# Roots by small steps on GpSimd, no product part in a short turn, and turned tokens cast by VectorE, in the second layer of a gated cross-attention block

## The reference

```python
def _L1_xattn_ref(x, context, Wq, Wk, Wv):      # 32 heads of 8
    def _rmsnorm(t):
        return t * jax.lax.rsqrt(jnp.mean(t * t, axis=-1, keepdims=True) + 1e-6)
    q = x @ Wq.T
    k_raw, v_raw = context @ Wk.T, context @ Wv.T
    ...
    q, k = _rmsnorm(q), _rmsnorm(k)
    attn = jax.nn.softmax(jnp.einsum('bhnd,bhmd->bhnm', q, k) * 8 ** -0.5, axis=-1)
    return jnp.einsum('bhnm,bhmd->bhnd', attn, v)
```

## Time and profile before

| | |
|---|---|
| median of three runs | 1718.73 us (1718.09 to 1726.04) |
| profiled execution | 1721.58 us, its span 1719.8 us |
| TensorE (PE) busy | 1616.0 us, 94% of the span |
| VectorE (DVE) busy | 1393.7 us, 81% |
| ScalarE (ACT) busy | 1381.0 us, 80% |
| GpSimd (POOL) busy | 1273.5 us, 74% |
| mean granted TensorE clock | 0.983 |
| feed-forward stage and first tiles | about 1200 to 1302 us |
| layer 1's attention and last half | 1302 us to the end |

### The profile page before, as it was taken

One profiled execution on the slowest core, in us unless ns is written; L12 is line 12 of the kernel. 1 busy time (PEld: TensorE's weight loads), 2 busy tenths in 40 slices (PEclk: granted clock), 3 DMA queues, 4 the chain that ended last, 5 costly groups with the idle time before them and its releaser, 6 DMA issues. The chain is left out here.

```text
span 1719.8 us, 43340 instructions
## 1 busy us (share of the span) xinstructions
PE 1616.0 (94%) x16022; PEld 1011.1 (59%) x16022; DVE 1393.7 (81%) x3487; ACT 1381.0 (80%) x2317; POOL 1273.5 (74%) x1170
## 2 busy tenths in 40 slices
PE   3799999999999999999999999988998999999997
PEld 1466777767776677767777777766553333333332
DVE  8889999999999989999888888889995755555422
ACT  4688888788888788888888888873337999999996
POOL 3558778787787877887877787765896989989400
PEclk9899999999999999999999999998999999999998
DMA  4299989999999999999989999996323232222100
GB/s 175 87 177 203 195 206 205 195 205 222 202 189 200 190 198 185 224 211 207 196 194 218 217 194 209 211 186 175 104 44 108 44 77 39 44 39 45 26 14 14
DMA packets 608867, 261.07 MB, mean 152 GB/s; under 512 B 576528, under 2 KB 581648, under 8 KB 607248
## 3 DMA queue, kind: packets, MB, share of 16 engines
q1 hardware_dynamic: 604432, 258.05, 70.3%
q10 hardware_dynamic: 4224, 0.25, 0.2%
HBM read 99.15 MB, written 17.29 MB: 68 GB/s over the span
## 5 line engine op out<-in xcount | busy, mean ns | idle before, releaser
L1750 PE MATMUL pv<-PT,VV 128*128 128x256 bf16 (+1 forms) x2880 | 340.6, 275 | 12.1 <-DMA PT<-PB 12.1
L1730 PE MATMUL score<-KK,QT 128*128 128x512 bf16 (+2 forms) x1920 | 341.5, 322 | 6.5 <-DVE mxp L1225 6.5
L2316 POOL TENSOR_TENSOR l_rr<-l_rr,mhalf 128x32 f32<-128x32 f32 (+1 forms) x60 | 333.2, 5553 | 5.0
L1490 ACT ACTIVATE PB<-S,rsum 128x1024 bf16<-128x1024 f32 (+1 forms) x256 | 246.5, 988 | 106.0 <-DVE rsum L1256 81.6
L1750 PEld LDWEIGHTS pv<-PT,VV 128*128 128x128 bf16 (+1 forms) x2880 | 280.7, 99 | 79.9 <-issue 31.8
L1247 DVE SCALAR_TENSOR_TENSOR PB<-S,rsum,PB 128x1024 bf16<-128x1024 f32 (+1 forms) x256 | 297.6, 1163 | 3.1 <-ACT PB L1490 3.1
L1730 PEld LDWEIGHTS score<-KK,QT 128*128 128x128 bf16 x1920 | 158.1, 98 | 144.0 <-DVE mxp L1225 12.6
L1480 ACT ACTIVATE S<-S,nmx 128x1601 f32<-128x1601 f32 x128 | 210.2, 1643 | 7.2 <-DVE nmx L1237 7.0
L2582 ACT ACTIVATE P<-score 128x1024 f32<-128x1024 f32 x196 | 199.1, 1060 | 12.6 <-PE score L2674 5.9
L1068 POOL TENSOR_SCALAR S<-S,rsum 128x256 f32<-128x256 f32 x128 | 73.1, 571 | 129.8 <-DVE rsum L1256 116.2
L2694 PE MATMUL pv<-P,V 128*9 128x256 f32 (+1 forms) x2288 | 154.2, 384 | 3.8 <-DVE pv L2120 2.4
(11 more groups left out here) (264 smaller groups left out, 3577.6 us busy)
## 6 DMA issues: line engine op xcount, KB each, us to landing
x<-rs_d SPq DMA_DIRECT2D x16, 936.0 KB, 5.3
rsb<-rs_d SPq DMA_DIRECT2D x16, 936.0 KB, 5.5
wsb<-w_split SPq DMA_DIRECT2D x46, 256.0 KB, 4.7
wsb<-w_split SPq DMA_DIRECT2D x23, 512.0 KB, 4.9
wpr<-in_wprojT SPq DMA_DIRECT2D x23, 512.0 KB, 6.5
context_d<-stage SPq DMA_DIRECT2D x16, 400.2 KB, 3.7
l_ctx<-context_d SPq DMA_DIRECT2D x4, 1601.0 KB, 7.2
rawh<-in_w_all SPq DMA_DIRECT2D x12, 512.0 KB, 5.5
```

Source lines behind the costliest of these rows:

```text
L1490: e.activation(m.PB[n % 2][:, 2 * a:a + b], m.S32[n % 2][:, a:b], ACT.Copy, scale=m.rsum[n % 2][:, 1:2]).then_inc(s["p_hi"], 1)
L1730: i = e.matmul(m.score[:, at:at + b - a], qt[:, kind, qp, q * P:(q + 1) * P], kk[:, kp, a:b], start=(k == 0), stop=(k == 2))
L1750: i = e.matmul(m.pv[:, at:at + 256], vv[0:rows, v, t, :], m.PT[k % 2][0:rows, turned(c, a), :], start=(c == first and r == 0), stop=(c == ...
L2316: e.tensor_tensor(rr, rr, m.mhalf[0:rows, 0:NH1], ALU.pow).then_inc(s["l1_rr"], 1)
```

## The change

1. POOL's root (60 tiles). Before: a tensor_scalar (mean square plus epsilon) and a tensor_tensor with `pow` and -0.5. After: the first tensor_scalar into x, a guess from the bits of x read as int32 (times -0.5 plus a constant, written as int32), and two refining steps, in all five tensor_scalar and seven tensor_tensor on [rows, 32] of float32, each waiting for the one before it. The small powers of the layer norms (lines 506 and 2309) stay.
2. `l1_slots`: the parts that fell into a short turn go to the turn behind it. Odd context tiles: parts in 7j + 5, 7j + 7, 7j + 7 (two in one turn). Tokens: tile 0 turns in turn 3, parts 4 and 5; tile 1 turns in turn 6, both parts in 7. The stack is now four turns behind the last part: 7j + 8 for even, 7j + 11 for odd context tiles, 9 and 11 for the tokens.
3. `last_turns`: the products of the last half at 11 and 12 in place of 12 and 13.
4. The cast of turned tokens of batches 1 to 3 moves from ScalarE to VectorE, straight ahead of the difference.

```diff
+def off_tail(n):
+    return n + (n % L1U == L1U - 1)
+
+def product_turns(c):
+    if c < TB:
+        return ((4, 5), (7, 7))[c]
+    first = L1U * (c // 2) + (5 if c % 2 else 2)
+    return tuple(off_tail(first + i) for i in range(3))
+
 def l1_slots(n):
     out = []
     for c in range(L1C):
-        first = 3 + 3 * c if c < TB else L1U * (c // 2) + (5 if c % 2 else 2)
+        turns = product_turns(c)
         parts = ("begin", "product") if c < TB else PARTS
-        if c < TB and n == first - 1:
+        if c < TB and n == turns[0] - 1:
             out.append(("turn_x", c))
-        if first <= n < first + len(parts):
-            out.append((parts[n - first], c))
-        if n == first + len(parts) + 4:
+        for part, turn in zip(parts, turns):
+            if n == turn:
+                out.append((part, c))
+        if n == turns[-1] + 4:
             out.append(("stack", c))
     return out
...
+GUESS = float(0x5F3759DF)
+NORM_STEPS = 10
+
+def pool_inverse_root(e, m, s, k, rows):
+    x, y = m.l1_nx[0:rows, :], m.l1_rr[k % 3][0:rows, :]
+    a, z = m.l1_na[0:rows, :], m.l1_nz[0:rows, :]
+    at = NORM_STEPS * k
+    e.wait_ge(s["l1_rr"], k)
+    e.tensor_scalar(x, m.l1_ss[k % 3][0:rows, :], 1.0 / D1, EPS6, ALU.mult, ALU.add).then_inc(s["l1_rr0"], 1)
+    e.wait_ge(s["l1_rr0"], k + 1)
+    if k >= 3:
+        e.wait_ge(s["l1_hd"], k - 2)
+    e.tensor_scalar(y.bitcast(I32), x.bitcast(I32), -0.5, GUESS, ALU.mult, ALU.add).then_inc(s["l1_newton"], 1)
+    e.wait_ge(s["l1_newton"], at + 1)
+    e.tensor_tensor(a, y, y, ALU.mult).then_inc(s["l1_newton"], 1)
+    e.wait_ge(s["l1_newton"], at + 2)
+    e.tensor_tensor(a, a, x, ALU.mult).then_inc(s["l1_newton"], 1)
...
+    e.tensor_scalar(z, a, 0.375, -1.25, ALU.mult, ALU.add).then_inc(s["l1_newton"], 1)
...
+    e.tensor_tensor(z, z, a, ALU.mult).then_inc(s["l1_newton"], 1)
...
+    e.tensor_scalar(z, z, 1.875, None, ALU.add).then_inc(s["l1_newton"], 1)
...
+    e.tensor_tensor(y, y, z, ALU.mult).then_inc(s["l1_newton"], 1)
...
+    e.tensor_tensor(a, y, y, ALU.mult).then_inc(s["l1_newton"], 1)
...
+    e.tensor_tensor(a, a, x, ALU.mult).then_inc(s["l1_newton"], 1)
...
+    e.tensor_scalar(a, a, -0.5, 1.5, ALU.mult, ALU.add).then_inc(s["l1_newton"], 1)
+    e.wait_ge(s["l1_newton"], at + 10)
+    e.tensor_tensor(y, y, a, ALU.mult).then_inc(s["l1_rr"], 1)
...
 def pool_prepare(e, m, s, b, what, c):
-        e.tensor_scalar(rr, ss, 1.0 / D1, EPS6, ALU.mult, ALU.add).then_inc(s["l1_rr0"], 1)
-        e.wait_ge(s["l1_rr0"], k + 1)
-        e.tensor_tensor(rr, rr, m.mhalf[0:rows, 0:NH1], ALU.pow).then_inc(s["l1_rr"], 1)
+        pool_inverse_root(e, m, s, k, rows)
...
 def dve_prepare(e, m, s, b, what, c):
     elif what == "turn_x":
+        if b:
+            e.wait_ge(s["xt_full"], TB * b + c + 1)
+            q = TB * b + c - 1
+            e.wait_ge(s["l1_pa"], place(q // TB, q % TB) + 1)
+            e.tensor_copy(m.l1_xT[:, 0, :, :].rearrange("p i t -> p (i t)"),
+                          x_bank(m, b)[:, 0:IC * P]).then_inc(s["xT_hi"], 1)
         e.wait_ge(s["xT_hi"], TB * b + c + 1)
...
-    return tuple(2 * L1U * b + n for n in (2, 4, 10, 12, 13))
+    return tuple(2 * L1U * b + n for n in (2, 4, 10, 11, 12))
...
 def act_prepare(e, m, s, b, what, c):
-    if what == "turn_x":
+    if what == "turn_x" and b == 0:
```

More of the change, by code:

```diff
@@ L9 @@
 I16 = mybir.dt.int16
+I32 = mybir.dt.int32
 ALU = mybir.AluOpType
@@ L84 @@
 xst_done xmv_done xrs_eps xrs_done xn_done xt_full xT_hi xT_lo
-l1_pa l1_kn l1_sq l1_ss l1_rr0 l1_rr l1_pv0 praw_in   l1_v l1_hd l1_s0 stack_up
+l1_pa l1_kn l1_sq l1_ss l1_rr0 l1_rr l1_newton l1_pv0 praw_in   l1_v l1_hd l1_s0 stack_up
 stack_in0 stack_in1 l1_s l1_exp l1_pv l1_os l1_ot l1_den l1_att l1_added
@@ L257, in allocate @@
             m.l1_sq = sb(c, "l1_sq", [P, H], F32)
+            m.l1_nx = sb(c, "l1_nx", [P, NH1], F32)
+            m.l1_na = sb(c, "l1_na", [P, NH1], F32)
+            m.l1_nz = sb(c, "l1_nz", [P, NH1], F32)
             m.l1_ss = [sb(c, f"l1_ss{i}", [P, NH1], F32) for i in range(3)]
@@ L2301, in sp_last @@
         e.dma_start(m.out[t * P:(t + 1) * P, :], m.x[:, t, :]).then_inc(s["out_done"], 16)
+GUESS = float(0x5F3759DF)
[14 more added lines that the diff above has]
+    e.tensor_tensor(a, a, x, ALU.mult).then_inc(s["l1_newton"], 1)
+    e.wait_ge(s["l1_newton"], at + 3)
+    e.tensor_scalar(z, a, 0.375, -1.25, ALU.mult, ALU.add).then_inc(s["l1_newton"], 1)
+    e.wait_ge(s["l1_newton"], at + 4)
+    e.tensor_tensor(z, z, a, ALU.mult).then_inc(s["l1_newton"], 1)
+    e.wait_ge(s["l1_newton"], at + 5)
+    e.tensor_scalar(z, z, 1.875, None, ALU.add).then_inc(s["l1_newton"], 1)
+    e.wait_ge(s["l1_newton"], at + 6)
+    e.tensor_tensor(y, y, z, ALU.mult).then_inc(s["l1_newton"], 1)
+    e.wait_ge(s["l1_newton"], at + 7)
+    e.tensor_tensor(a, y, y, ALU.mult).then_inc(s["l1_newton"], 1)
+    e.wait_ge(s["l1_newton"], at + 8)
+    e.tensor_tensor(a, a, x, ALU.mult).then_inc(s["l1_newton"], 1)
+    e.wait_ge(s["l1_newton"], at + 9)
+    e.tensor_scalar(a, a, -0.5, 1.5, ALU.mult, ALU.add).then_inc(s["l1_newton"], 1)
+    e.wait_ge(s["l1_newton"], at + 10)
+    e.tensor_tensor(y, y, a, ALU.mult).then_inc(s["l1_rr"], 1)
 def pool_prepare(e, m, s, b, what, c):
@@ L2311, in pool_prepare @@
         k, rows = place(b, c), l1_rows(c)
-        ss, rr = m.l1_ss[k % 3][0:rows, :], m.l1_rr[k % 3][0:rows, :]
         e.wait_ge(s["l1_ss"], k + 1)
-        e.tensor_scalar(rr, ss, 1.0 / D1, EPS6, ALU.mult, ALU.add).then_inc(s["l1_rr0"], 1)
-        e.wait_ge(s["l1_rr0"], k + 1)
-        e.tensor_tensor(rr, rr, m.mhalf[0:rows, 0:NH1], ALU.pow).then_inc(s["l1_rr"], 1)
+        pool_inverse_root(e, m, s, k, rows)
 def pool_layer1(e, m, s):
@@ L2558, in act_prepare @@
 def act_prepare(e, m, s, b, what, c):
-    if what == "turn_x":
[L2560 to L2563, removed]
+    if what == "turn_x" and b == 0:
+        e.wait_ge(s["xt_full"], c + 1)
+        if c:
+            e.wait_ge(s["l1_pa"], place(0, c - 1) + 1)
         e.copy(m.l1_xT[:, 0, :, :].rearrange("p i t -> p (i t)"), x_bank(m, b)[:, 0:IC * P]).then_inc(s["xT_hi"], 1)
```

## The result

Twenty-two runs of each kernel on the same chip give a median of 1723.94 us after (1717.37 to 1729.44) and 1718.78 before (1712.77 to 1726.22): ratio 1.0028, 95% interval 1.0017 to 1.0038. The change makes the kernel slower by some 5 us; 4 us less was forecast. The number lies in the range, on the wrong side of no change.

The account below looks back on a forecast made before the run. VectorE was taken to bound the feed-forward stage, TensorE the middle of layer 1's batches. Terms summed to -4.2 us: 1717.4 profiled, less 2.85 a median of 1714.5; own range 1708 to 1721, 8 in 10 within 1701 to 1731.

Parts of the forecast that it names:

- (a): POOL's root: 3.9 us against 5.8; at the feed-forward stage's end ScalarE's 3.12 wait mostly goes: -3.1.
- R2: Layer 1's root: twelve operations at 0.43 each, some 5.9 us beside VectorE, even stack waits: 1734; chance 0.16.
- R3: Feed-forward stage: VectorE held by POOL, +6 us in place of +0.5, thus 1720; chance 0.08.
- +0.5: Feed-forward stage: VectorE held by POOL's small operations, +0.5 us, bounds 0 and 6.
- b: Cast of turned tokens to VectorE: -1.4 us in batch 0's first group, -1.8 over two later batches.
- (d): Short turn: TensorE's small waits on ScalarE go, some 0.2 us a group; -1.2 for groups 1 and 7.
- (e): VectorE's order: even stack ahead of l_att makes TensorE late, +0.37 us net, 15 times: +5.6, bounds 0 and 13.
- c: Last tile's stack of a batch: TensorE's 2.29 us wait in batch 3 keeps perhaps 0.5: -1.8.
- f: Last products leave turn 13 for 12 and 11: -1.0 us in all, bounds 0 and -2.5.
- R1: VectorE's order costs nothing, l_att in time: -3 us in place of +5.6, clock perhaps staying up: 1703; chance 0.26.

Follow-up runs that it names:

- the root alone: The kernel before with only the root by twelve small operations; slots, stacks, last turns and cast as before: 1715.75 us, ratio 0.9964.
- the later stacks: The changed kernel with all stacks one turn later, five turns behind the last part in place of four: 1709.65 us, ratio 0.9925 to the kernel before.
- the power kept: The changed kernel with the power of before in place of the small steps; slots, order and cast as changed: 1786.02 us, ratio 1.0376.

## Why the prediction was wrong

**Right.** (a) The root: 3.9 us alone and 4.5 beside a stack were forecast; in mid-batch POOL's roots take 3.81 for even tiles (from the first instruction to the end of the last) and 4.54 for odd ones; in the feed-forward stage their median is 4.9, where 4.8 was forecast. The int32 operation is a row like the others (0.22 at its shortest), so the cause that R2 names falls. Its sign, VectorE waiting for l1_rr in mid-batch, came all the same, with small steps that are small (below). The memset was to come some 3.5 earlier and came 3.85 earlier. R3 falls: 89.1 us from layer 0's end to the first exponential both times; a few rows grew by 0.09 (squares of up to 0.50), and nothing came of it, so the +0.5 was 0. What the clock would do stood open, and it fell all the same. POOL's busy time in the middle is 27.04, not 35: the gaps between the twelve operations don't count as busy. By groups:

```
                                           forecast   measured
feed-forward stage (held VectorE)            +0.5        0
first group of batch 0 (a, b)                -4.5       -3.6
groups 0 and 1 of batches 1, 2 (b, d)        -2.2       -1.6
batch 0, groups 1 to 7 (d, e)                +1.5       +6.5
batches 1, 2, groups 2 to 7 (d, e)           +3.3       +3.1
batch 3 (c, f)                               -2.8       -2.3
sum                                          -4.2       +2.1
```

(The forecast's rows are its terms put where it had them; 0.2 of (d) is in each of groups 1 and 7.) One row near its forecast is so by luck: in batches 1 and 2 the first groups gain 1.8 and 1.7, where 0.9 was forecast, and the second lose 1.0, where 0.2 was to be gained. Of the single terms: the root alone gives 2.8 in batch 0's first group, where 3.1 was forecast for the stage's end, and 1.6 in batch 3, where 1.8 was; the cast is worth 2.7 us, 0.3 of it in batch 0, where 1.4 was forecast, and 2.4 in batches 1 and 2, where a part of 1.8 was; the last products 0.5, where 1.0 was; the slots 0.32 a group (12.59 to 12.27), where 0.2 was, but the changed kernel gets none of it.

**The step that failed** is the term of (e) and its list of places. The mechanism is the one foreseen: the stack ahead of `third`, TensorE waiting for l_att, 19 times, and +0.37 net a group was +0.27. (Group 7 of batches 0 to 2 waits too, 0.53, and takes 0.16 more than before, where 0.2 less was forecast.) But I worked it out from one group of batch 1 and multiplied by 15. In batch 0, VectorE has the weights' steps as well, up to 2.28 us, and they stand in front of the root on POOL and the stack on VectorE: 3.6 of the 5.0 us by which batch 0 missed are shown to be theirs, and group 1's belong there by its rows, with TensorE waiting for V as well as for l_att. The prediction named POOL being held by VectorE for 0.45 and stopped there; it never asked what the longest VectorE instruction near a root is, though the trace of before has the row of 1326.16 with its 2.18. Before, the stack had one turn of slack that swallowed most of this: batch 0's groups 2 to 5 were 0.4 over the others in all.

**The second omission** is the odd tile. I checked that the even root is in time (5.0 allowed, 4.5 needed; true) and not the odd one. Its stack at the fourth turn waits 2.45 for the root in the steady groups of batches 1 and 2, and the next copy of V is behind it. In steady groups that costs 0.1; wherever a root is late it costs more: 6.7 us in all, the tokens' stacks included.

**Measured against what was possible,** the error is larger than 6 us. The earlier stack costs 15.3. The even tiles' 8.7 of it lie between the bounds 0 and 13 that I gave (e), though (e) was counted from groups of 12.59; the other 6.7 had no term. TensorE at 12.59 was not the floor: ScalarE's fourteen exponentials, 12.27, are, and the slots reach it once the wait is gone. R1, the same change with l_att in time, was priced at 1703, 15.7 below before, 3 of it for a clock that stays up. The kernel with the later stacks is that case, and 0.9925 is 12.9 below; its granted clock did fall (0.50 from 1302 to 1304 us), and without those 3 the price was 12.8. That the two agree so well is luck in part: its single terms were off either way. R2 priced a root of 5.9 beside VectorE at 16 us in layer 1, from even tiles; with the power kept the cost was 61, with the odd tile's wait and the clock in it. The result itself lies within 0.5% of no change, the likeliest of the three outcomes.

## What to carry to other kernels

When an entry is moved a turn ahead in the program of an engine that runs in order, price what it is now in front of and, separately, what it now waits for; do it for every kind of turn (even, odd, first, last) and for the batch with extra work, not for one clean group times a count. A faster helper engine is worth what its result's deadline lets it be: the same root was worth 5.8 us in the old schedule and 14.8 in the new one with the later stacks. And if a change mixes a latency cut with a tighter schedule, try the schedule one notch looser first: here that notch was 15 us.

## What the runs showed that was not expected

- One small POOL instruction can last as long as the VectorE instruction that it meets: 2.19 and 2.21 us for an operation of 0.22, beside a VectorE operation of 2.28 in SBUF that began 0.15 to 0.17 ahead (rows of 1321.14 and 1315.56 above). The trace of before has it too (2.18, 1326.16 us). Roots by small steps that meet such an operation take 5.85 to 6.49 us; the power itself lasted 5.43 to 5.97.
- The other way the two are not alike: the longest of VectorE's squares took 0.50 in place of 0.41 in the feed-forward stage, and the gate kept its 0.69 within a power of 5.43.
- Between layer 0's end and the first exponential four of the runs' profiles have 87.5 us, not 89.1: the first two steps of the feed-forward stage behind layer 0's end take 9.1 to 9.2 in place of 10.8. Two executions with the same code there have one and the other, so it is no difference between kernels; its cause was not looked for.
- Layer 0's end varies by up to 9 us between executions, whatever the kernel. Two single profiled executions of kernels 5 us apart stood in the wrong order because of it.
